# Turning most parts of H tiles 0 and 1 by DMA, and finding maxima over partitions with a TensorE transpose, in a quantised gated block

## The chip, the core and the metric

The kernel runs on one core of one Trainium2 chip. The metric is the device time of one execution in microseconds (us), lower is better. The engines are called here as the profile calls them: PE is the matrix engine, DVE the vector engine, ACT the scalar engine, POOL is GpSimd, SP issues all the DMAs. "SPq" is SP's queue; "PEld" is PE's loading of weights, which overlaps its matmuls.

## What is computed

```
x = x + tanh(g_xattn) * matmul(fake_quant(layernorm(x)), fake_quant(ctx))
h_in2 = layernorm(x)                               # 1024 rows x 1024
A, g  = quant_act(h_in2); Wg, Wu = quant_w(w_gate), quant_w(w_up)
h     = silu(A @ Wg.T * g) * (A @ Wu.T * g)        # 1024 rows x 2752
Am, gm = quant_act(h); Wd = quant_w(w_down)
x = x + tanh(g_ffn) * (Am @ Wd.T * gm)

def quant_act(v):            # blocks of 16 columns, fp8 rounding
    g = max(max|v| / (448 * 6), 1e-8)              # one maximum over the whole tensor
    vr = (v / g)[:, reorder]                       # the index may be the identity
    normal, last = vr[:, :-128], vr[:, -128:]
    q1 = fp8_block(last); q2 = fp8_block(last - q1)   # outliers in two steps
```

Two things matter here. quant_act needs one maximum over all elements before any element can be rounded, and each rounded tile has to be turned (rows to columns) before PE can multiply it.

## The kernel before, in words

The work goes in three stretches. The opening (to about 267 us of the span) does the attention part, quantises the activations and the first weights. The loop (to about 645 us) multiplies gate and up, makes h in units of 256 columns and stores it to DRAM (`h_d`), while the weights for the third stretch are quantised and turned into `big` (`wd_hi`, `wd_lo`). The last stretch, called here the down stretch, takes h back tile by tile: an H tile is 128 rows by 2752 columns, there are 8 of them, and tiles use two buffers in turn (`h_in[:, 0]`, `h_in[:, 1]`).

For each H tile, in the down stretch:
- `coef_unbound`, `keep_h_outliers` and `scale_h` (DVE, lines 1409, 1410, 1462, 1466) prepare one factor and one scale per block of 16.
- the tile is multiplied by its factors: by DVE part by part for tiles 0 and 1 (line 1477), by POOL in one go for tiles 2 to 7 (`h_times_coef`, line 626, after `hcoef_ready`).
- rounding (`start_part`, `end_part`): line 1478 makes a power of two `mg` from each element with integer operations, line 1479 keeps `mg` above a floor, lines 1485 and 1486 round by adding `mg` and taking it away, and line 1487 multiplies by the scale. The last part of a tile has the outliers as well (`quantise_twice`, twelve short instructions from line 1268 to 1275).
- the tile is split into two f16 numbers (hi and lo) and turned. Tiles 0 and 1 are cut in six parts of 3 or 4 blocks of 128 columns (`H_PARTS`). A part is turned by PE in f32 into a PSUM bank (`turn_h`, line 892), ACT copies it out as hi (`hi_part`, line 708), DVE takes hi from it and writes lo (`lo_part`, line 1178). Tiles 2 to 7 go in two halves of 11 blocks: ACT writes hi (line 838) and DVE lo (`lo_half`, line 1504) side by side in `nat_h`, and one DMA per half turns both (`turn_half`, line 503) into `amT`.
- PE multiplies each turned block three times (hi hi, hi lo, lo hi) for each of two halves of the output (`down`, line 1001): 132 matmuls of 128x512 per tile, 1056 in all. DVE adds the result to x1 (`finish`, line 1513, two instructions per tile), and SP stores it.

Each engine takes its instructions in the order in which they are written. DVE's order for tiles 0 and 1 is: start of part c, `lo_group` of part c-1, end of part c. For tiles 2 to 7: preparation, lo of the second half of the tile before, `finish(t-2)`, start and end of half 0, start of half 1, lo of half 0, end of half 1. PE's order is: turn the next part after the first output half of the present one. In the down stretch nothing but these orders and the semaphores decides what runs when.

The maximum over the whole tensor is found in three places with `partition_all_reduce` on POOL: for the flags that say whether an index is the identity (line 557), for the activations (line 568, then DVE line 1219) and for h (line 620, then DVE line 1434). Before each, DVE has one number per partition (`nfl`, `gmx`); after each, every partition has the maximum.

## Time and profile before

| | |
|---|---|
| median of 3 runs | 915.83 us (915.15 to 916.29) |
| the profiled execution | 915.4 us, of which the span from first to last instruction is 913.6 us |
| PE busy / DVE busy | 84% / 73% of the span |
| ACT, POOL busy | 29%, 36% |
| mean granted TensorE clock | 0.935 of full speed |

The shares are means over three stretches that have different limits. In the loop PE is busy without a gap, so it sets the time there; in the opening PE is seldom busy and DVE mostly is; the down stretch has both kinds of time in it. Granted clock 1.00 is 2.4 GHz, 0.50 is 1.2 GHz.

### The profile page before, as it was taken

To read this page: it belongs to the slowest core of one execution; us is meant where nothing else is said; L and a number is where in the kernel's file an instruction comes from. 1 tells how busy PE (TensorE), PEld (TensorE's weight loads), DVE (VectorE), ACT (ScalarE), POOL (GpSimd) and SP (SyncE) were. 2 spreads that over 40 slices of the span, in tenths; PEclk is the share of its full clock that TensorE was granted. 3 is DMA by queue.
4 is the path that set the end of the run, shared out by engine and by line. 5 is a ranking of instruction groups with operands and counts; after the bars stand their busy time and mean duration, and the time that the engine had idled before them with its cause. 6 is when DMAs were issued, how large, how long until landed. Compare 5 with 4: busy or idle time off the path is not lost.

```text
span 913.6 us, 10781 instructions
## 1 busy us (share of the span) xinstructions
PE 765.4 (84%) x3676; PEld 362.1 (40%) x3676; DVE 669.3 (73%) x1054; ACT 263.0 (29%) x344; POOL 328.0 (36%) x173
## 2 busy tenths in 40 slices
PE   0689200579999999999999999999699579999998
PEld 0233100445554444444444444444245234444443
DVE  5999789988757575757667576732787899999950
ACT  1973420331334342425343343420001001101010
POOL 1001136745216475757575665820000222012200
PEclk9999555689999999999999999999799879999999
DMA  7633300110036978898797979753100244764440
GB/s 289 215 103 155 117 21 0 47 56 21 28 111 121 237 161 200 181 211 188 182 207 170 232 166 237 159 116 136 68 31 33 85 101 126 171 171 125 101 110 24
DMA packets 178854, 119.01 MB, mean 130 GB/s; under 512 B 151808, under 2 KB 163072, under 8 KB 177792
## 3 DMA queue, kind: packets, MB, share of 16 engines
q1 hardware_dynamic: 178816, 118.53, 51.1%
q8 instruction: 20, 0.33, 0.1%
q14 instruction: 18, 0.15, 0.1%
HBM read 61.88 MB, written 19.66 MB: 89 GB/s over the span
## 4 chain that ended last, share of the span: by engine, by line
PE 70%; DVE 22%; issue 2%; ACT 2%; POOL 1%; DMA 1%; SPq 0%; DVEq 0%; ACTq 0%
PE acc L950 45%; PE acc L1001 22%; PE tb L892 2%; DVE bst L1070 2%; DVE big L1245 1%; DVE wbuf L1172 1%; DVE h_in L1244 1%; DVE h_in L1243 1%; PE acc L878 1%; DVE big L1100 1%; DVE h_in L1190 1%; DVE wbuf L1504 1%; DVE mid L1144 1%; DVE wbuf L1142 1%; DVE w_max L1160 1%
## 5 line engine op out<-in xcount | busy, mean ns | idle before, releaser
L950 PE MATMUL acc<-mid 128*128 128x512 f16 (+1 forms) x2112 | 448.9, 376 | 0.0
L950 PEld LDWEIGHTS acc<-mid 128*128 128x128 f16 x2112 | 207.5, 98 | 239.7 <-issue 2.7
L1001 PE MATMUL acc<-big,mid 128*128 128x512 f16 x1056 | 234.0, 383 | 17.1 <-DMA mid<-wbuf 15.8
L563 POOL TENSOR_TENSOR wbuf<-wbuf,w_inv 128x1024 f32<-128x1024 f32 (+1 forms) x68 | 128.5, 1894 | 157.6 <-DVE w_inv L1166 157.6
L1001 PEld LDWEIGHTS acc<-big,mid 128*128 128x128 f16 x1056 | 103.9, 99 | 142.4 <-issue 20.4
L602 POOL TENSOR_TENSOR h_in<-wbuf,h_in 128x1024 f16<-128x1024 f32 (+1 forms) x56 | 114.5, 2044 | 86.7 <-ACT h_in L799 86.5
L1316 DVE SCALAR_TENSOR_TENSOR h_out<-acc,gs,silu 128x256 f32<-128x256 f32 (+1 forms) x88 | 41.5, 471 | 114.0 <-ACT silu L757 87.7
L702 ACT ACTIVATE wbuf<-wbuf 128x1024 f32<-128x1024 f32 (+1 forms) x68 | 69.1, 1017 | 100.6 <-POOL wbuf L563 99.8
L1160 DVE TENSOR_REDUCE tb<-wbuf 128x64 f32<-128x1024 f32 (+1 forms) x56 | 65.5, 1169 | 43.3 <-DMA wbuf<-in_L_ffn_w_gate_dram 24.1
L626 POOL TENSOR_TENSOR h_in<-h_in,mid 128x2752 f32<-128x2752 f32 x6 | 29.3, 4885 | 181.5 <-DVE mid L1542 181.5
L799 ACT ACTIVATE h_in<-wbuf 128x1024 f16<-128x1024 f32 (+1 forms) x56 | 57.1, 1019 | 115.2 <-DVE wbuf L1172 115.2
L757 ACT ACTIVATE silu<-acc,gs 128x256 f32<-128x256 f32 (+1 forms) x88 | 40.1, 456 | 88.0 <-PE acc L950 88.0
L1172 DVE SCALAR_TENSOR_TENSOR wbuf<-wbuf,tb 128x1024 f32<-128x1024 f32 (+1 forms) x56 | 65.2, 1163 | 0.3
L838 ACT ACTIVATE wbuf<-h_in 128x1408 f16<-128x1408 f32 x12 | 16.5, 1377 | 149.1 <-DVE h_in L1487 88.9
L892 PE MATMUL tb<-ident,big 128*128 128x128 f32 x64 | 11.2, 349 | 56.9 <-DVE big L1275 50.8
L708 ACT ACTIVATE mid<-tb 128x512 f16<-128x512 f32 (+2 forms) x52 | 28.0, 575 | 97.0 <-PE tb L892 75.0
L1504 DVE TENSOR_TENSOR wbuf<-h_in,wbuf 128x1408 f16<-128x1408 f32 x12 | 42.3, 3528 | 1.8 <-ACT wbuf L838 1.4
L1178 DVE TENSOR_TENSOR mid<-tb,mid 128x512 f16<-128x512 f32 (+2 forms) x52 | 32.3, 654 | 12.4 <-ACT mid L708 12.2
L1321 DVE TENSOR_REDUCE hm<-h_out 128x256 f32 (+2 forms) x88 | 34.0, 387 | 2.7
L878 PE MATMUL acc<-mid,big 128*128 128x512 bf16 x128 | 31.2, 400 | 5.1 <-DVE big L1100 5.1
L892 PEld LDWEIGHTS tb<-ident,big 128*128 128x128 f32 x64 | 10.1, 184 | 57.7 <-DVE big L1275 51.3
L1166 DVE RECIPROCAL w_inv<-tb 128x64 f32<-128x64 f32 (+1 forms) x56 | 30.2, 539 | 1.9
(150 smaller groups left out, 595.2 us busy)
## 6 DMA issues: line engine op xcount, KB each, us to landing
h_in<-h_d SPq DMA_DIRECT2D x8, 1376.0 KB, 7.0
wbuf<-in_L_ffn_w_gate_dram SPq DMA_DIRECT2D x21, 512.0 KB, 4.5
wbuf<-in_L_ffn_w_up_dram SPq DMA_DIRECT2D x21, 512.0 KB, 4.1
h_d<-h_out SPq DMA_DIRECT2D x80, 128.0 KB, 3.4
wbuf<-in_L_ffn_w_down_dram SPq DMA_DIRECT2D x16, 512.0 KB, 4.4
wbuf<-in_ctx_dram SPq DMA_DIRECT2D x12, 512.0 KB, 4.7
big<-in_x_dram SPq DMA_DIRECT2D x8, 512.0 KB, 7.6
x_d<-big SPq DMA_DIRECT2D x8, 512.0 KB, 4.2
```

Of the source, the lines that this page charges most:

```text
L563: pool.tensor_tensor(w, w, spread(w_inv[0:rows, b, 0:cols // BLK]), ALU.mult).then_inc(w_scaled, 1)
L602: pool.tensor_tensor(nat[s % 4][:, H:H + cols], wbuf[:, s % 4, 0:cols], nat[s % 4][:, 0:cols], ALU.subtract)\
L702: act.activation(wbuf[0:rows, b, 0:cols], wbuf[0:rows, b, 0:cols], ACT.Copy, bias=MAGIC, scale=W_UP)\
L757: act.activation(silu[:, m % 2, 0:cols], acc[m % 4][:, 0:cols], ACT.Silu, scale=gs[:, 2:3]).then_inc(silu_done, 1)
L799: act.activation(nat[s % 4][:, 0:cols], wbuf[:, s % 4, 0:cols], ACT.Copy).then_inc(nat_hi, 1)
L878: pe.matmul(acc[pair(t) + hf][:], aT[:, k, t * P:(t + 1) * P], ctxq[:, b * KT + k, hf * MW:(hf + 1) * MW], start=(k == 0), stop=False)
L950: last = pe.matmul(acc[m % 4][:, 0:cols], left[:, k, s * P:(s + 1) * P], ring[:, slot, right, k, 0:cols], start=(k == 0 and left is a_hi a ...
L1001: last = pe.matmul(acc[2 * i + hf][:], amT[:, i, k // DH, left, k % DH, :], right[:, k, hf * MW:(hf + 1) * MW], start=(k == 0 and left == ...
L1160: dve.tensor_reduce(top, blocks(wbuf[0:rows, b, 0:cols]), AX_X, ALU.max, apply_absolute_value=True).then_inc(scale_step, 1)
L1172: dve.scalar_tensor_tensor(out=w, in0=w, scalar=MAGIC, in1=spread(block_scale(b, looped)[0:rows, 0:cols // BLK]), op0=ALU.subtract, op1=AL ...
L1316: dve.scalar_tensor_tensor(out=h_out[:, m % 2, 0:cols], in0=acc[m % 4][:, cols:2 * cols], scalar=gs[:, 2:3], in1=silu[:, m % 2, 0:cols], o ...
L1504: dve.tensor_tensor(nat_h[:, g, 1, :], h_in[:, i, g * DH * P:(g + 1) * DH * P], nat_h[:, g, 0, :], ALU.subtract)\
```

## The change

It has three parts.

1. `H_PARTS` becomes a list over all tiles: tile 0 in the same six parts as before, tile 1 in four parts of 5, 6, 5 and 6 blocks, tiles 2 to 7 in halves as before. Only the first two parts of tile 0 are still turned by PE (`PE_PARTS`). The other eight of tiles 0 and 1 are written as hi (ACT) and lo (DVE) into `nat_h`, and SP turns each with two DMAs (`turn_part`), one for hi and one for lo.
2. The floor on `mg` moves from DVE to ACT for all tiles: ACT computes Relu(mg * 2^20 - floor) in place (`floor_magic`), and DVE's two rounding instructions add the floor back. With that, the factors lose a power of two and the scales change their sign. In tiles 2 to 7 DVE's `finish(t-2)` now stands behind the start of half 0 and no longer before it.
3. The three calls of `partition_all_reduce` go. PE transposes the column of 128 numbers, spread over 128 columns, into a PSUM bank (`spread_max`), so that every partition has all 128 numbers, and DVE takes their maximum (one reduce). For the flags, DVE does this behind the first layernorm and no longer ahead of the work on the parameters.

POOL still multiplies H tiles 2 to 7.

```diff
-H_PARTS = (0, 3, 7, 11, 15, 19, DK)
-DG = len(H_PARTS) - 1
+H_CUTS = ((0, 3, 7, 11, 15, 19, DK), (0, 5, DH, 16, DK)) + ((0, DH, DK),) * (NT - 2)
+H_PARTS = [(t, slice(a, b)) for t, cuts in enumerate(H_CUTS) for a, b in zip(cuts, cuts[1:])]
+PE_PARTS = 2
+HALVES = sum(1 for t, ks in H_PARTS if t < 2)
...
+MAGIC_FLOOR = 1.5 * V_UP * 2.0**-6
...
@@ sync @@
+            def turn_part(n):
+                t, ks = H_PARTS[n]
+                sp.wait_ge(nat_h_lo, n - PE_PARTS + 1)
+                for v in range(2):
+                    sp.dma_start_transpose(turned_part(t, v, ks), nat_part(v, ks)).then_inc(part_turned[n], 16)
...
-            for t in range(2):
-                sp.wait_ge(turned, (t + 1) * DG + G_DOWN)
-                load_tile(t + 2, t)
+            for n in range(PE_PARTS, HALVES):
+                turn_part(n)
+                t, ks = H_PARTS[n]
+                if ks.stop == DK:
+                    sp.wait_ge(turned, G_DOWN + PE_PARTS)
+                    load_tile(t + 2, t)
...
@@ gpsimd: three calls go @@
-            pool.wait_ge(flag_step, 4)
-            pool.partition_all_reduce(nall[:], nfl[:], P, RMAX).then_inc(flag_step, 1)
...
-            pool.wait_ge(part_max, 1)
-            pool.partition_all_reduce(gall[:, 0:1], gmx[:, 0:1], P, RMAX).then_inc(all_max, 1)
...
-            pool.wait_ge(part_max, 2)
-            pool.partition_all_reduce(gall[:, 1:2], gmx[:, 1:2], P, RMAX).then_inc(all_max, 1)
...
@@ scalar @@
+            def floor_magic(n, ks):
+                mg = mgh[:, 0:min(ks.stop * P, I) - ks.start * P]
+                act.wait_ge(magic_made, n + 1)
+                act.activation(mg, mg, ACT.Relu, bias=floor_bias[:, 0:1], scale=V_UP).then_inc(magic_floor, 1)
+            floor_magic(0, H_PARTS[0][1])
+            for n, (t, ks) in enumerate(H_PARTS):
+                if n < PE_PARTS:
+                    hi_part(G_DOWN + n, (G_DOWN + n) % 4, turned_part(t, 0, ks), ks.stop - ks.start, P)
+                else:
+                    if n == PE_PARTS:
+                        act.wait_ge(nat_lo, UNITS_D * UNIT_PIECES)
+                    act.wait_ge(am_ready, n + 1)
+                    g = ks.start // DH
+                    if t in (1, 2) and ks.start == g * DH:
+                        for m in parts_in(t - 1, g):
+                            if m >= PE_PARTS:
+                                act.wait_ge(part_turned[m], 32)
+                    elif t > 2:
                         act.wait_ge(h_turned[g], 16 * (t - 2))
-                    act.activation(nat_h[:, g, 0, :], h_in[:, t % 2, g * DH * P:(g + 1) * DH * P], ACT.Copy).then_inc(nat_h_hi, 1)
+                    act.activation(nat_part(0, ks), h_in[:, t % 2, ks.start * P:ks.stop * P], ACT.Copy).then_inc(nat_h_hi, 1)
+                if n + 1 < len(H_PARTS):
+                    floor_magic(n + 1, H_PARTS[n + 1][1])
...
@@ tensor @@
+            def spread_max(column, out):
+                return pe.transpose(out, column.to_broadcast([P, P]), ident[:])
...
+            pe.wait_ge(flag_step, 4)
+            for i in range(2):
+                last = spread_max(nfl[:, i:i + 1], tb[3][:, i * P:(i + 1) * P])
+            last.then_inc(flag_step, 1)
...
+            pe.wait_ge(part_max, 1)
+            pe.wait_ge(lo_done, G_PRE)
+            spread_max(gmx[:, 0:1], tb[3][:, 0:P]).then_inc(all_max, 1)
...
+            pe.wait_ge(part_max, 2)
+            spread_max(gmx[:, 1:2], tb[3][:, 0:P]).then_inc(all_max, 1)
+            turn_h(0)
+            for n, (t, ks) in enumerate(H_PARTS):
+                if n < PE_PARTS:
+                    pe.wait_ge(lo_done, G_DOWN + n + 1)
+                elif t < 2:
+                    pe.wait_ge(part_turned[n], 32)
+                else:
+                    if ks.start == 0:
+                        pe.wait_ge(y_out, t - 1)
+                    pe.wait_ge(h_turned[ks.start // DH], 16 * (t - 1))
+                for hf in range(2):
+                    last = down(t % 2, hf, range(ks.start, ks.stop))
+                    if ks.stop == DK:
+                        last.then_inc(y_done, 1)
+                    if hf == 0 and n + 1 < PE_PARTS:
+                        turn_h(n + 1)
...
@@ vector @@
-            dve.wait_ge(flag_step, 5)
-            dve.tensor_copy(flag[:], nall[:]).then_inc(flags_ready, 1)
...
+            dve.wait_ge(flag_step, 5)
+            step(dve.tensor_reduce(nall[:], tb[3][:, 0:2 * P].rearrange("p (n c) -> p n c", n=2), AX_X, ALU.max))
+            dve.tensor_copy(flag[:], nall[:]).then_inc(flags_ready, 1)
...
+            step(dve.tensor_reduce(gall[:, 1:2], tb[3][:, 0:P], AX_X, ALU.max))
...
-                step(dve.tensor_scalar(mg.bitcast(I32), v.bitcast(I32), 0x7F800000, 0x00400000, ALU.bitwise_and, ALU.bitwise_or))
-                step(dve.tensor_scalar(mg, mg, 1.5 * V_UP * 2.0**-6, None, ALU.max))
-            def end_part(t, i, ks):
+                dve.tensor_scalar(mg.bitcast(I32), v.bitcast(I32), 0x7F800000, 0x00400000, ALU.bitwise_and, ALU.bitwise_or).then_inc(magic_made, 1)
+            def end_part(n, i, ks):
                 cs = slice(ks.start * P, min(ks.stop * P, I))
                 v, mg = h_in[:, i, cs], mgh[:, 0:cs.stop - cs.start]
-                step(dve.scalar_tensor_tensor(out=v, in0=v, scalar=1.0 / V_UP, in1=mg, op0=ALU.mult, op1=ALU.add))
-                step(dve.tensor_tensor(v, v, mg, ALU.subtract))
+                dve.wait_ge(magic_floor, n + 1)
+                step(dve.scalar_tensor_tensor(out=v, in0=mg, scalar=MAGIC_FLOOR, in1=v, op0=ALU.add, op1=ALU.add))
+                step(dve.scalar_tensor_tensor(out=v, in0=mg, scalar=MAGIC_FLOOR, in1=v, op0=ALU.add, op1=ALU.subtract))
...
+            def lo_h(n):
+                t, ks = H_PARTS[n]
+                if n < PE_PARTS:
+                    g = G_DOWN + n
+                    lo_part(g, g % 4, turned_part(t, 0, ks), turned_part(t, 1, ks), ks.stop - ks.start, P)
+                else:
+                    dve.wait_ge(nat_h_hi, n - PE_PARTS + 1)
+                    dve.tensor_tensor(nat_part(1, ks), h_in[:, t % 2, ks.start * P:ks.stop * P], nat_part(0, ks), ALU.subtract)\
+                        .then_inc(nat_h_lo, 1)
...
+            for n, (t, ks) in enumerate(H_PARTS):
                 i = t % 2
-                reorder_max(t, i)
-                coef_unbound(t, i, step)
-                keep_h_outliers(i)
-                dve.tensor_scalar(h_coef[:, i, :], h_coef[:, i, :], gs[:, 6:7], None, ALU.min).then_inc(hcoef_ready, 1)
-                scale_h(t, i)
-                if t == 2:
-                    lo_group(1, DG - 1)
+                if ks.start == 0:
+                    reorder_max(t, i)
+                    if t >= 1:
+                        if t >= 2:
+                            coef_unbound(t, i, step)
+                        keep_h_outliers(i)
+                        if t >= 2:
+                            dve.tensor_scalar(h_coef[:, i, :], h_coef[:, i, :], gs[:, 6:7], None, ALU.min).then_inc(hcoef_ready, 1)
+                        scale_h(t, i)
+                    if t >= 2:
+                        lo_h(n - 1)
+                if t == 0 and ks.stop == DK:
+                    keep_h_outliers(0)
+                start_part(t, i, ks)
+                if n == 0:
+                    dve.tensor_scalar(gs[:, 5:6], gs[:, 3:4], th[:, 1:2], W_DOWN, ALU.mult, ALU.mult)
+                    step(dve.tensor_scalar(gs[:, 7:8], gs[:, 4:5], -1.0 / FP8_MAX, None, ALU.mult))
+                    dve.wait_ge(hmax_done, (NU + 1) * NT)
+                    scale_h(0, 0)
+                elif t < 2 or ks.start > 0:
+                    lo_h(n - 1)
                 else:
-                    lo_half(t - 1, 1 - i, 1)
-                finish(t - 2, i)
-                start_part(t, i, slice(0, DH))
-                end_part(t, i, slice(0, DH))
-                start_part(t, i, slice(DH, DK))
-                lo_half(t, i, 0)
-                end_part(t, i, slice(DH, DK))
-            lo_half(NT - 1, 1, 1)
+                    finish(t - 2, i)
+                end_part(n, i, ks)
+            lo_h(len(H_PARTS) - 1)
```

What the order of instructions is on DVE in the middle of tile 0 (the part of blocks 7 to 10; `mid` is `mg` or `amT`, `tb` is the PSUM bank of the turned part), before:

```order
L1477 SCALAR_TENSOR_TENSOR h_in<-mid,gs,h_in 128x512
L1478 TENSOR_SCALAR mid<-h_in 128x512 [waits dve_step]
L1479 TENSOR_SCALAR mid<-mid 128x512 [waits dve_step]
L1178 TENSOR_TENSOR mid<-tb,mid 128x512 [waits hi_done,dve_step]
L1485 SCALAR_TENSOR_TENSOR h_in<-h_in,mid 128x512
L1486 TENSOR_TENSOR h_in<-h_in,mid 128x512 [waits dve_step]
L1487 TENSOR_TENSOR h_in<-h_in,mid 128x512 [waits dve_step]
```

and now:

```order
L1530 SCALAR_TENSOR_TENSOR h_in<-mid,gs,h_in 128x512
L1531 TENSOR_SCALAR mid<-h_in 128x512 [waits dve_step]
L1555 TENSOR_TENSOR wbuf<-h_in,wbuf 128x512 [waits nat_h_hi]
L1538 SCALAR_TENSOR_TENSOR h_in<-mid,h_in 128x512 [waits magic_floor]
L1539 SCALAR_TENSOR_TENSOR h_in<-mid,h_in 128x512 [waits dve_step]
L1540 TENSOR_TENSOR h_in<-h_in,mid 128x512 [waits dve_step]
```

One instruction of the part is gone (line 1479), the lo instruction reads `h_in` and `wbuf` in place of a PSUM bank, and the rounding waits for ACT (`magic_floor`).

On DVE from the preparation of tile 2 to its first rounding, before:

```order
L1409 TENSOR_SCALAR mid<-hm 128x172
L1410 RECIPROCAL mid<-mid 128x172 [waits dve_step]
L1462 TENSOR_SCALAR mgo_a<-h_in,gs 128x128 [waits dve_step]
L1542 TENSOR_SCALAR mid<-mid,gs 128x172 [waits dve_step]
L1466 TENSOR_SCALAR mid<-hm,gs 128x172
L1178 TENSOR_TENSOR mid<-tb,mid 128x384 [waits hi_done,dve_step]
L1513 SCALAR_TENSOR_TENSOR mid<-acc,gs,mid 128x512 [waits y_done,x1_loaded0]
L1513 SCALAR_TENSOR_TENSOR mid<-acc,gs,mid 128x512 [waits y_done]
L1478 TENSOR_SCALAR mid<-h_in 128x1408 [waits h_scaled]
L1479 TENSOR_SCALAR mid<-mid 128x1408 [waits dve_step]
L1485 SCALAR_TENSOR_TENSOR h_in<-h_in,mid 128x1408 [waits dve_step]
```

and now:

```order
L1461 TENSOR_SCALAR mid<-hm 128x172
L1462 RECIPROCAL mid<-mid 128x172 [waits dve_step]
L1515 TENSOR_SCALAR mgo_a<-h_in,gs 128x128 [waits dve_step]
L1577 TENSOR_SCALAR mid<-mid,gs 128x172 [waits dve_step]
L1519 TENSOR_SCALAR mid<-hm,gs 128x172
L1555 TENSOR_TENSOR wbuf<-h_in,wbuf 128x768 [waits nat_h_hi,dve_step]
L1531 TENSOR_SCALAR mid<-h_in 128x1408 [waits h_scaled]
L1564 SCALAR_TENSOR_TENSOR mid<-acc,gs,mid 128x512 [waits y_done,x1_loaded0]
L1564 SCALAR_TENSOR_TENSOR mid<-acc,gs,mid 128x512 [waits y_done]
L1538 SCALAR_TENSOR_TENSOR h_in<-mid,h_in 128x1408 [waits magic_floor]
```

The lo instruction of tile 1's last part (line 1178 before, 1555 now) is larger and has two inputs in SBUF, and `finish` (1513 before, 1564 now) has moved behind the first instruction that waits for POOL (`h_scaled`).

On PE from the end of the loop to tile 0's second part, before:

```order
L892 MATMUL tb<-ident,h_in 128x128 x3
L1001 MATMUL acc<-big,mid 128x512 x9
L892 MATMUL tb<-ident,h_in 128x128 x4
L1001 MATMUL acc<-big,mid 128x512 x21
L892 MATMUL tb<-ident,h_in 128x128 x4
L1001 MATMUL acc<-big,mid 128x512 x24
L892 MATMUL tb<-ident,h_in 128x128 x4
```

and now:

```order
L883 MATMUL tb<-ident,gmx 128x128
L934 MATMUL tb<-ident,h_in 128x128 x3
L1051 MATMUL acc<-big,mid 128x512 x9
L934 MATMUL tb<-ident,h_in 128x128 x4
L1051 MATMUL acc<-big,mid 128x512 x1047
```

The transpose of the maxima stands ahead, two turns of parts are left of twelve, and all other matmuls of the stretch stand in one row.

## Rows read from the trace of the kernel before

**Rows 1.** The page: costliest groups, busy us and mean ns, idle before and its releaser.

```profile
L1001 PE MATMUL acc<-big,mid 128*128 128x512 f16 x1056 | 234.0, 383 | 17.1 <-DMA mid<-wbuf 15.8
```

**Rows 2.** Stretches before tile 2's matmuls: busy us, clock, DMA share, GB/s.

```profile
core 0: us, PE busy (x) PEld busy (x) DVE busy (x) ACT busy (x) POOL busy (x), PEclk, DMA share, GB/s
...
682.00:714.00 32.00, 30.79 (x153) 15.24 (x152) 26.59 (x56) 3.37 (x6) 0.00 (x0) 1.00 0.12 45
714.00:736.00 22.00, 6.75 (x33) 2.87 (x31) 18.67 (x20) 1.87 (x2) 4.89 (x1) 0.71 0.43 123
```

**Rows 3.** Waits, 640 to 760 us: total us, times, longest.

```profile
PE acc L1001 <- DMA mid<-wbuf: 15.8, 2, 15.5
...
DVE mid L1178 <- ACT mid L708: 9.2, 10, 1.7
```

**Rows 4.** Timeline (start us, us): the maximum of h and the first parts.

```profile
646.66 0.16 DVE L1418 TENSOR_REDUCE gmx<-gpart 128x1 f32<-128x4 f32 x1
...
647.37 0.15 DVE L1434 TENSOR_SCALAR gs<-gall 128x1 f32<-128x1 f32 x1 [0.23 <-POOL gall L620]
...
651.46 0.56 DVE L1487 TENSOR_TENSOR h_in<-h_in,mid 128x384 f32<-128x384 f32 x1
...
652.27 0.87 PE L892 MATMUL tb<-ident,h_in 128*128 128x128 f32 x3 [7.18 <-DVE h_in L1487]
...
654.38 4.01 PE L1001 MATMUL acc<-big,mid 128*128 128x512 f16 x9 [1.25 <-DVE mid L1178]
```

**Rows 5.** Groups by shape on DVE, 640 to 720 us: busy us, mean ns.

```profile
L1485 DVE SCALAR_TENSOR_TENSOR h_in<-h_in,mid 128x512 f32<-128x512 f32 x8 | 5.5, 682 | 0.0
L1479 DVE TENSOR_SCALAR mid<-mid 128x512 f32<-128x512 f32 x8 | 3.4, 427 | 0.3
...
L1479 DVE TENSOR_SCALAR mid<-mid 128x384 f32<-128x384 f32 x2 | 0.7, 361 | 0.1
```

**Rows 6.** Timeline: tile 2 from DVE's first instruction to its matmuls.

```profile
713.60 0.25 DVE L1409 TENSOR_SCALAR mid<-hm 128x172 f32<-128x172 f32 x1
...
715.87 4.89 POOL L626 TENSOR_TENSOR h_in<-h_in,mid 128x2752 f32<-128x2752 f32 x1 [68.53 <-DVE mid L1542]
716.03 0.56 DVE L1178 TENSOR_TENSOR mid<-tb,mid 128x384 f16<-128x384 f32 x1
...
720.79 0.89 DVE L1478 TENSOR_SCALAR mid<-h_in 128x1408 int32<-128x1408 int32 x1 [2.88 <-POOL h_in L626]
...
722.65 1.63 DVE L1485 SCALAR_TENSOR_TENSOR h_in<-h_in,mid 128x1408 f32<-128x1408 f32 x1
...
727.69 1.38 ACT L838 ACTIVATE wbuf<-h_in 128x1408 f16<-128x1408 f32 x1 [12.89 <-DVE h_in L1487]
...
731.00 3.31 SPq L503 DMA_TRANSPOSE mid<-wbuf  x1
...
736.28 16.31 PE L1001 MATMUL acc<-big,mid 128*128 128x512 f16 x66 [15.54 <-DMA mid<-wbuf]
```

**Rows 7.** Timeline: lo of tile 2's second half beside POOL, and PE afterwards.

```profile
741.21 4.88 POOL L626 TENSOR_TENSOR h_in<-h_in,mid 128x2752 f32<-128x2752 f32 x1 [20.45 <-DVE mid L1542]
741.38 6.19 DVE L1504 TENSOR_TENSOR wbuf<-h_in,wbuf 128x1408 f16<-128x1408 f32 x1
...
752.86 37.51 PE L1001 MATMUL acc<-big,mid 128*128 128x512 f16 x173 [0.27 <-DMA mid<-wbuf]
```

**Rows 8.** DMA issues: operation, times, median us from issue to landing.

```profile
big<-h_in SPq DMA_TRANSPOSE x48, 3.8
```

**Rows 9.** Timeline of the opening.

```profile
4.64 3.97 SPq L327 DMA_DIRECT2D big<-in_x_dram x8
...
9.45 0.17 DVE L1052 CAST flag<-nall 128x2 int32<-128x2 f32 x1 [2.87 <-POOL nall L557]
...
10.91 9.58 DVE L1070 BATCH_NORM_STATS2 bst<-big 128x6 f32<-128x512 f32 x16
```

**Rows 10.** The last two of the eight loads of x: us from issue to landing.

```profile
DMA to landing us min/median/max: 9.5/9.9/10.3
```

More of the change, by code:

```diff
@@ L29 @@
 AX_X = mybir.AxisListType.X
-RMAX = bass.bass_isa.ReduceOp.max
 P = 128
@@ L265, in gated_block @@
         am_ready = sem("am_ready")
+        magic_made = sem("magic_made")
+        magic_floor = sem("magic_floor")
         nat_h_hi = sem("nat_h_hi")
         nat_h_lo = sem("nat_h_lo")
+        part_turned = [sem(f"part_turned{n}") for n in range(HALVES)]
         h_turned = [sem(f"h_turned{g}") for g in range(2)]
@@ L301, in unit_tile, with part_of, parts_in, nat_part @@
             return u * NT + (2 * NT + s)
-        def halves_before(t):
-            return 2 * (t - 2)
-        def parts_before(t):
-            return DG * t if t < 2 else 2 * DG + halves_before(t)
+        def part_of(t, k):
+            return next(n for n, (at, ks) in enumerate(H_PARTS) if at == t and ks.start <= k < ks.stop)
+        def parts_in(t, g):
+            return [n for n, (at, ks) in enumerate(H_PARTS) if at == t and ks.start // DH == g]
+        def nat_part(v, ks):
+            g = ks.start // DH
+            return nat_h[:, g, v, (ks.start - g * DH) * P:(ks.stop - g * DH) * P]
+        def turned_part(i, v, ks):
+            g = ks.start // DH
+            return amT[:, i, g, v, ks.start - g * DH:ks.stop - g * DH, :]
         def loads_before(b, u):
@@ L989, in _, with turn_h @@
                     unit(2 * it + (jj + 1), 1 - jj)
-            def turn_h(t, c):
-                pe.wait_ge(am_ready, t * DG + c + 1)
-                g = G_DOWN + t * DG + c
-                turn_piece(h_in[:, t, :], P, range(H_PARTS[c], H_PARTS[c + 1]), g, g % 4)
+            def turn_h(n):
+                pe.wait_ge(am_ready, n + 1)
+                t, ks = H_PARTS[n]
+                turn_piece(h_in[:, t, :], P, range(ks.start, ks.stop), G_DOWN + n, (G_DOWN + n) % 4)
             def down(i, hf, ks):
@@ L1218, in _ @@
             dve.wait_ge(all_max, 1)
+            step(dve.tensor_reduce(gall[:, 0:1], tb[3][:, 0:P], AX_X, ALU.max))
             step(dve.tensor_scalar(gs[:, 0:1], gall[:, 0:1], 1.0 / GDIV, TINY, ALU.mult, ALU.max))
@@ L1408, in coef_unbound @@
                 mx, coef = hm[:, t, :], h_coef[:, i, :]
-                link(dve.tensor_scalar(coef, mx, H_SMALL, 1.0 / (FP8_MAX * V_UP), ALU.max, ALU.mult))
+                link(dve.tensor_scalar(coef, mx, H_SMALL, 1.0 / FP8_MAX, ALU.max, ALU.mult))
                 link(dve.reciprocal(coef, coef))
@@ L1464, in scale_h @@
             def scale_h(t, i):
-                step(dve.tensor_scalar(h_scale[:, i, :], hm[:, t, :], gs[:, 7:8], TINY, ALU.mult, ALU.max))
+                step(dve.tensor_scalar(h_scale[:, i, :], hm[:, t, :], gs[:, 7:8], -TINY, ALU.mult, ALU.min))
             def start_part(t, i, ks):
```

68 lines of the change are left out of this document (8 added, 60 removed).

## The prediction

> **What bounds the kernel now.** I read the page first, then the waits and the stretches of the down part, then its timeline. The group of line 1001 on the page holds all 1056 matmuls of the down stretch, and its idle time has one main cause, a DMA that turns H [rows 1]. The waits say that this is two waits, one of 15.5 us [rows 3]. The stretch from 714 to 736 us shows it: PE is busy for 6.75 of 22 us while DVE is busy for 18.67 [rows 2]. From 752.86 on PE runs at 37.51 / 173 = 0.217 us per matmul and does not wait again before the end [rows 7]. So the end follows from the moment at which the second half of tile 2 reaches PE, 752.86, and everything ahead of that in the down stretch is a race for it.
>
> Who runs that race is seen in the timeline of tile 2 [rows 6]. PE starts tile 2 when a DMA lands, that DMA is issued behind DVE's lo, and DVE's chain for tile 2 starts at 713.60, right behind its work on tiles 0 and 1. PE had nothing to do by then. So the sum is made along DVE: how much earlier does it come to 713.60, and how much earlier to the issue at 731.00? The second half follows the first at the same distance, since between them stand the same outliers, the same preparation of tile 3 and the same POOL instruction. What DVE saves inside tile 2 and later, beyond that point, only makes tiles wait for PE.
>
> **The change part by part.**
>
> *DVE's waits for turned parts.* In tiles 0 and 1 DVE waits ten times for ACT's hi, 9.2 us in all [rows 3], because PE turns a part only between the matmuls of the part before. Eight of ten such parts no longer pass PE: hi comes from ACT straight from `h_in`, and DVE has the next part's first two instructions in between. Laying the instructions of both engines one behind the other with the durations of the rows, I get for what is left: 0.6 and 1.8 at the two parts that PE still turns, and where ACT has copy and floor to do in one part, 0.1 to 0.5 each until the floor is there (0.60 + 0.1 for a floor of 512 columns, estimated from ACT's 1.38 for 1408 [rows 6]), 1.9 together. So 4.3 stay and **4.9** go. Bounds: none of the 1.9 stays (6.8), or each floor takes 0.4 longer and all of it shows (about 1.3).
>
> *The floor.* Twelve instructions of line 1479 leave DVE in tiles 0 and 1: eight at 0.43, two at 0.36, two a little shorter [rows 5], each with 0.03 to the next: **5.2**. The two rounding instructions keep their size; one changes from two to three operands, and line 1485, which is of that form, takes 0.68 for 512 [rows 5], as the other does within 0.01.
>
> *Six parts into four in tile 1.* Line 1485 takes 0.68 for 512 and 1.63 for 1408 columns [rows 5, 6], so 1.06 ns per column and 0.14 fixed. Two parts fewer with six instructions each save about **1.8**, with bounds 1.2 and 2.4.
>
> Together DVE comes to tile 2 some 11.9 us earlier, at 701.7 by the old clock.
>
> *Around tile 2's factors.* POOL multiplies for 4.89, and DVE then had 2.88 idle, because lo (0.56) and `finish` lay in POOL's shadow [rows 6]. Now the lo of tile 1's last part has two inputs in SBUF. What that does beside POOL is seen at tile 2's second half: lo of 1408 columns, alone no longer than a rounding instruction of that size (1.63), takes 6.19 and ends 1.48 behind POOL [rows 6, 7]; the 0.56 one that reads PSUM ran at full speed beside POOL [rows 6]. So the new one, of 768 columns, ends 0.9 behind POOL: **+0.8**, and if it were free, 0. The Trainium skill ("SBUF — State Buffer", section "SBUF: two separate sides") has the same as a rule: GpSimd and a DVE instruction with two SBUF inputs exclude each other for a whole instruction, which speaks against this part of the change. By the rule the term is 0.8, by sizes alone it would be nothing and the time 0.8 lower; the trace agrees with the rule.
>
> `finish` now stands between the start and the end of half 0. It takes 1.3 there, then some 0.3 until the floor is ready, and the 0.93 of line 1479 are gone: **+0.7**, between 0.4 and 1.2. For the lo of half 0, DVE waits for ACT's copy where it had line 1479 to do; that is even within 0.1. From 11.9 the gain shrinks to 10.4.
>
> *The maximum of h.* From the end of `gmx` (646.82) to DVE's next instruction took 0.55 with POOL [rows 4]. Now: DVE to PE 0.25, as between 652.02 and 652.27; one f32 transpose, bounded by the 0.87 of three [rows 4], say 0.45; a reduce of 128 numbers and the semaphores 0.35. That makes 1.05, so **+0.5**, with bounds 0 and +1.0. The maximum of the activations, in the opening's chain, costs the same once more: **+0.5**.
>
> *The opening.* DVE waited 2.87 for POOL's answer on the flags ahead of anything on x, then ran sixteen statistics without a gap from 10.91 to 20.49, 1.2 per tile, the last tile from 19.3. That tile's load was issued at 8.2 and took 10.3 [rows 9, 10], so it is there at 18.5 and the statistics can end 0.8 earlier. The flags' reduce falls into a wait for ACT behind the layernorm. **-0.8**, between 0 and -0.85.
>
> *The turns as DMAs.* A pair of DMA transposes with 6 or 8 blocks each lands 3.8 after its issue in the median of single ones [rows 8], and 44 blocks in one DMA took 5.3 (731.00 to 736.28) [rows 6]. I take 4.0 for a pair of 4 to 6 blocks, bounds 2.7 and 5.3. They are on PE's path, not DVE's. PE will wait for parts: for the third part of tile 0 about 2 us, for the first of tile 1 some 2 to 4 (its lo comes behind tile 0's outliers, and its DMAs are issued behind the load of H tile 2 on SP's queue), and for the last of tile 1, whose lo ends behind POOL at 710.3 (701.7 + 0.5 for the maximum, 2.3 to POOL's start, 4.9, and 0.9). That one lands at 714.3, its 36 matmuls end at 722.1. Tile 2 lands at 736.3 - 10.4 + 0.5 = 726.4. So PE still waits 4.3 there, and that cover hides the turns' cost; beyond it, each us costs one. The transposes that leave PE (0.15 each) save nothing for the same reason.
>
> Sum: -4.9 - 5.2 - 1.8 + 0.8 + 0.7 + 0.5 + 0.5 - 0.8 = -10.2. The profiled execution took 915.4 (span 913.6), 0.4 under the median of the runs, so 905.2, or 905.6 from the median. I put 905.4.
>
> **The rivals.**
>
> *The floor on ACT comes late (0.14).* The Trainium skill ("ScalarE: Activation LUTs", "Rules for kernel authors") sends relu and max to VectorE; its figures, an estimate of 0.3 + 0.83 ns per element, make 0.7 for a floor of 512 columns. The sum above has nearly that already. The mechanism goes by rows: line 1479 takes 0.43 on DVE [rows 5], ACT needs 1.38 for 1408 in its plain copy [rows 6], and in each part it has both the copy and the floor, in a row. If a floor with its two hand-overs takes 0.4 more than I took, nine of them lie open up to tile 2's first rounding: +3.6, 909. For it: ACT's floor reads its bias from memory. Against: ACT is nearly idle here.
>
> *PE becomes the bound in tiles 0 and 1 (0.12).* After a wait PE's clock falls: the nine matmuls at 654.38 took 0.446 each, against 0.217, behind 7 us of little work [rows 4, 7], so a restart costs 2.0. One restart at the last part of tile 1 moves 722.1 to 724.1, still inside the cover. With pairs that land at 5.3 and two restarts that add up it is 727 to 729: +1 to +3, 906 to 908.
>
> *The gain is larger (0.08).* No floor ever lies open and the maxima cost nothing: 1.9 + 1.0 more, 902.4.
>
> *Slower than before (0.04).* The short waits of PE in front of every part keep its clock at the lower level. All 255 matmuls behind the first nine would take 0.446 in place of 0.217, 58 us more. It needs less: when about 120 of them do, tile 1 ends 27 us late, at 749, PE takes up tile 2 some 13 us later than before, at full clock its first half ends at 763.5 and not at 752.9, and the time is about 926. It decides from the point at which tile 1 ends after 738. Against it: from 682 to 714 PE was busy for 30.79 of 32 us, so it waited now and then, and kept 1.00 of the clock [rows 2].
>
> *Nothing changes (0.02).* Something that I don't see sets tile 2's landing, such as the load of H tile 2 or 3 behind the turns.
>
> **How the numbers follow.** The main case has 0.60 and, with its bounds added as they would fall together, reaches from 902.5 to 908. The range takes in the larger gain and the late floor: 901.5 to 909.5, which leaves out less than 2 in 10. A measurement of this kernel tells some 0.2% (1.8 us) from no change. Faster by over that: all cases but the last two, less a little for a mishap outside this list, 0.93; within 0.2%: 0.03; slower: 0.04.
>
> **What would show it.** Right: DVE starts tile 2 near 702, with no wait over 0.6 behind the second part of tile 0; the lo of tile 1's last part takes about 5.5 beside POOL; PE starts tile 2 near 726 after a wait of some 4 us, and is without a gap from about 742 on; the statistics end near 19.7; the two maxima take near 1.0. Wrong: DVE waiting for `magic_floor` over 0.5 a part, PE at the lower clock for most of tile 0 or 1, turn pairs that take over 5.3, or a gap of PE later than 745.

## The result, and the profile after

The changed kernel takes 901.47 us (median of 4 runs, 900.67 to 901.84); the kernel before took 916.06 in the same rounds. The ratio is 0.9841, with a 95% interval from 0.9824 to 0.9858: faster by 14.6 us. The prediction was 905.4 with a range from 901.5 to 909.5, so the sign was right, but the gain, forecast at 10.2, was 4.4 larger than said, and the measured time lies just under the lower end of the range. The profiled execution took 901.84, its span is 900.1 (before: 915.4 and 913.6).

I read the new page and the waits first. In the page's costliest groups (columns as in [rows 1]) the matmuls of the down stretch and the new floor on ACT read:

```profile
L1051 PE MATMUL acc<-big,mid 128*128 128x512 f16 x1056 | 235.6, 387 | 9.9 <-DMA mid<-wbuf 8.7
...
L852 ACT ACTIVATE mid<-mid,floor_bias 128x1408 f32<-128x1408 f32 (+7 forms) x22 | 24.7, 1124 | 56.4 <-DVE mid L1531 56.4
```

PE's idle time in the stretch fell from 17.1 [rows 1] to 9.9 us. The waits of the changed kernel between 640 and 760 us (as [rows 3]: in total, times, longest) say where it and DVE's waits went:

```profile
PE acc L1051 <- DMA mid<-wbuf: 8.7, 4, 3.6
...
DVE mid L1229 <- ACT mid L731: 2.7, 2, 2.3
...
DVE h_in L1538 <- ACT mid L852: 2.0, 8, 0.4
...
DVE wbuf L1555 <- ACT wbuf L871: 1.3, 2, 0.7
```

The one wait of 15.5 at tile 2 has become 3.6, beside three smaller ones in tiles 0 and 1, and DVE's ten waits for a turned part are two. The timeline of tile 2 (start and duration in us) answers to [rows 6]:

```profile
698.55 0.25 DVE L1461 TENSOR_SCALAR mid<-hm 128x172 f32<-128x172 f32 x1
...
700.81 4.88 POOL L649 TENSOR_TENSOR h_in<-h_in,mid 128x2752 f32<-128x2752 f32 x1 [103.14 <-DVE mid L1577]
700.98 5.52 DVE L1555 TENSOR_TENSOR wbuf<-h_in,wbuf 128x768 f16<-128x768 f32 x1
...
707.34 1.47 ACT L852 ACTIVATE mid<-mid,floor_bias 128x1408 f32<-128x1408 f32 x1 [7.84 <-DVE mid L1531]
708.84 1.63 DVE L1538 SCALAR_TENSOR_TENSOR h_in<-mid,h_in 128x1408 f32<-128x1408 f32 x1 [0.22 <-ACT mid L852]
...
710.67 7.94 PE L1051 MATMUL acc<-big,mid 128*128 128x512 f16 x36 [1.24 <-DMA mid<-wbuf]
...
716.94 3.30 SPq L525 DMA_TRANSPOSE mid<-wbuf  x1
```

DVE comes to tile 2 at 698.55, not at 713.60. To split that into opening and down stretch, I took the long last pieces of each kernel's chain of waits (start, us, and the matmuls run together). Before:

```profile
266.95 378.15 PE acc L950 x1752
...
752.86 156.88 PE acc L1001 x726
```

After:

```profile
264.07 378.15 PE acc L1000 x1752
...
722.23 173.95 PE acc L1051 x792
```

The long middle piece takes 378.15 in both and starts 2.9 earlier now. Before, PE's last wait ended at 752.86 [rows 7], 107.8 behind the end of the long piece (645.10); from there on the rest, 726 matmuls, takes 156.88. After, PE's last matmul ends at 896.18, so the same 726, at the same 156.88, begin at 739.3, 97.1 behind 642.22. So the spans' difference of 13.5 is **2.9 from the opening and 10.7 from the down stretch**. The forecast had -0.3 for the opening (-0.8 for the flags, +0.5 for the maximum of the activations) and -9.9 for the down stretch. The opening is what I got wrong. The split is good to less than a us only: in the nine kernels here that take both opening maxima on PE the long piece starts anywhere from 263.40 to 264.87, in the two that take both on POOL at 266.95 and 267.19.

### The profile page after: what moved, and what is told of

Read it like the earlier page. It is cut to its first block, busy times and chain, and to the rows that moved or that the text cites. A ratio compares the mean times of both kernels' runs of the same rounds, so it can differ in the third digit from the quotient of the medians.

```text
span 900.1 us, 10681 instructions
## 1 busy us (share of the span) xinstructions
PE 762.3 (85%) x3638; PEld 358.4 (40%) x3643; DVE 657.4 (73%) x1021; ACT 287.0 (32%) x364; POOL 326.1 (36%) x171
## 4 chain that ended last, share of the span: by engine, by line
PE 68%; DVE 24%; ACT 2%; issue 2%; DMA 2%; POOL 1%; SPq 1%; DVEq 0%; ACTq 0%
PE acc L1000 46%; PE acc L1051 20%; DVE bst L1118 2%; PE tb L934 2%; DVE big L1297 1%; DVE wbuf L1223 1%; DVE big L1148 1%; DVE h_in L1296 1%; DVE h_in L1241 1%; DVE w_max L1211 1%; DMA mid<-wbuf 1%; DVE h_in L1295 1%; DVE mid L1195 1%; DVE wbuf L1193 1%; DVE h_in L1539 1%
## 5 line engine op out<-in xcount | busy, mean ns | idle before, releaser
L1555 DVE TENSOR_TENSOR wbuf<-h_in,wbuf 128x1408 f16<-128x1408 f32 (+4 forms) x20 | 53.0, 2652 | 5.7 <-ACT wbuf L871 5.5
L871 ACT ACTIVATE wbuf<-h_in 128x1408 f16<-128x1408 f32 (+4 forms) x20 | 22.1, 1105 | 107.2 <-DVE h_in L1327 62.3
L852 ACT ACTIVATE mid<-mid,floor_bias 128x1408 f32<-128x1408 f32 (+7 forms) x22 | 24.7, 1124 | 56.4 <-DVE mid L1531 56.4
L731 ACT ACTIVATE mid<-tb 128x512 f16<-128x512 f32 (+2 forms) x42 | 22.4, 578 | 43.0 <-PE tb L979 21.7
L1564 DVE SCALAR_TENSOR_TENSOR mid<-acc,gs,mid 128x512 f32<-128x512 f32 x16 | 11.4, 739 | 31.0 <-PE acc L1051 31.0
```

What stands on the lines that cost most here:

```text
L1555: dve.tensor_tensor(nat_part(1, ks), h_in[:, t % 2, ks.start * P:ks.stop * P], nat_part(0, ks), ALU.subtract)\
```

## The experiments

Each kernel was timed in five rounds (4 to 8 executions) against the kernel before; gains are against the median of the kernel before in the same rounds (915.63 to 916.49). "Slower than the changed kernel" compares with its 901.47, which comes from other rounds; reckoned by the gains, such differences change by up to 0.4.

**The maxima.** First theory (P): something behind the removed `partition_all_reduce` of the activations was worth more than the reduce's own path. The kernel before with only this maximum moved to PE:

```diff
-            pool.wait_ge(part_max, 1)
-            pool.partition_all_reduce(gall[:, 0:1], gmx[:, 0:1], P, RMAX).then_inc(all_max, 1)
...
+            pe.wait_ge(part_max, 1)
+            pe.wait_ge(lo_done, G_PRE)
+            spread_max(gmx[:, 0:1], tb[3][:, 0:P]).then_inc(all_max, 1)
...
+            step(dve.tensor_reduce(gall[:, 0:1], tb[3][:, 0:P], AX_X, ALU.max))
```

> The kernel before, with only the maximum of the activations found by a TensorE transpose and a DVE reduce, in place of POOL's partition_all_reduce. Theory P (after a partition_all_reduce POOL cannot start its next ordinary instruction for some 7 us, and in the opening 2.9 us of that lie open): the path of the maximum is 0.3 longer, POOL starts its first product about 2.9 earlier, net about 2 us faster, 914. Rival Q (the gain in the opening comes from the earlier start, by which DVE and POOL meet otherwise): 0.3 slower, 916.4. The prediction's own term was 0.5 slower.

Measured: 914.2, ratio 0.9974 (0.9964 to 0.9985), a gain of 2.3 where the prediction had a loss of 0.5. Its long piece starts at 265.43, 1.5 earlier than before.

The changed kernel, with a `partition_all_reduce` of `gmx` into a column that nothing reads. It takes nothing away and nobody waits for its result; only POOL's order has one instruction more:

```diff
+            pool.wait_ge(part_max, 1)
+            pool.partition_all_reduce(unused[:, 0:1], gmx[:, 0:1], P, RMAX)
             for what, n in (("coef", 0), ("coef", 1), ("coef", 2), ("piece", 4), ("piece", 5), ("scale", 0), ("scale", 1),
```

> The changed kernel as it is, and POOL does a partition_all_reduce of the activation maxima as well, whose result nobody reads. The path of the maximum is untouched. Theory P: POOL's first product starts 2 to 3 us later and the end moves by about that, 903.5 to 904.4. Rival Q: nobody waits for it, 901.5.

Measured: 903.3 (0.9854, 0.9838 to 0.9869), 1.8 slower than the changed kernel. The timeline (idle before and its releaser in brackets) shows the mechanism; the kernel before:

```profile
121.44 0.38 POOL L568 PARTITION_ALL_REDUCE gall<-gmx  x1 [20.45 <-DVE gmx L1215]
128.95 6.16 POOL L576 TENSOR_TENSOR big<-big,h_in 128x1024 f32<-128x1024 f32 x3 [7.14 <-issue]
...
135.07 5.24 POOL L563 TENSOR_TENSOR wbuf<-wbuf,w_inv 128x1024 f32<-128x1024 f32 x2
...
138.45 2.42 DVE L1243 TENSOR_SCALAR h_in<-big 128x1024 int32<-128x1024 int32 x1
```

The changed kernel:

```profile
126.06 5.71 POOL L598 TENSOR_TENSOR big<-big,h_in 128x1024 f32<-128x1024 f32 x3 [26.03 <-DVEq L1348]
...
131.73 4.72 POOL L587 TENSOR_TENSOR wbuf<-wbuf,w_inv 128x1024 f32<-128x1024 f32 x2
...
137.45 0.68 DVE L1295 TENSOR_SCALAR h_in<-big 128x1024 int32<-128x1024 int32 x1
```

The changed kernel with the unused reduce:

```profile
120.56 0.38 POOL L612 PARTITION_ALL_REDUCE unused<-gmx  x1 [20.44 <-DVE gmx L1270]
128.00 6.16 POOL L600 TENSOR_TENSOR big<-big,h_in 128x1024 f32<-128x1024 f32 x3 [7.06 <-issue]
```

The reduce is shown with 0.38 us, but POOL's next instruction starts 7.1 behind its end, "issue" in the brackets: it waits for nothing that the profile shows. Its operands are ready long before (DVE makes the last coefficient at 125.61 in the changed kernel, and POOL starts at 126.06 there). In the kernels with the reduce POOL starts 1.9 to 2.3 later behind that coefficient than in the changed one. DVE meets this delay at its second bit operation (line 1243 before, 1295 after): before, POOL's pair of multiplications still runs beside it, until 140.31, and it takes 2.42; after, the pair is over at 136.45, and it takes 0.68. That 1.7 is the gain. A reduce that stands where POOL has nothing to do should cost nothing; the same unused instruction at the maximum of h:

```diff
+            pool.wait_ge(part_max, 2)
+            pool.partition_all_reduce(unused[:, 1:2], gmx[:, 1:2], P, RMAX)
             def h_times_coef(t, i):
```

> The changed kernel, and POOL does an unused partition_all_reduce of the h maxima, after which it is idle for some 57 us. Theory P: the gap behind it is covered by that idleness, 901.5. If a partition_all_reduce costs time whatever follows it, about 2 us more.

Measured: 901.49 (0.9839, 0.9825 to 0.9852): nothing. These are the same rounds as those of the 903.3, so the two unused reduces differ by 1.8 through their place alone. The same view of this kernel:

```profile
644.55 0.38 POOL L648 PARTITION_ALL_REDUCE unused<-gmx  x1 [46.45 <-DVE gmx L1475]
700.99 4.88 POOL L654 TENSOR_TENSOR h_in<-h_in,mid 128x2752 f32<-128x2752 f32 x1 [56.05 <-DVE mid L1582]
```

POOL idles 56 us behind it anyway. The flags, back on POOL in the changed kernel, with DVE's wait for them ahead of the statistics as before:

```diff
+            pool.wait_ge(flag_step, 4)
+            pool.partition_all_reduce(nall[:], nfl[:], P, RMAX).then_inc(flag_step, 1)
...
+            dve.wait_ge(flag_step, 5)
+            dve.tensor_copy(flag[:], nall[:]).then_inc(flags_ready, 1)
```

> The changed kernel with the flags' maximum back on POOL and ahead of DVE's work on the parameters. The statistics then end 0.8 later; if that reaches the end, 902.3. If the earlier start of DVE is swallowed later in the opening, 901.5.

Measured: 902.6 (0.9855, 0.984 to 0.987), 1.1 slower where the term says 0.8; its long piece starts at 265.21, also 1.1 later. Now all three maxima together, first moved alone in the kernel before:

> The kernel before, with all three maxima found by TensorE and DVE, and nothing else changed. Theory P: the opening gains 2.9, the maximum of h costs 0.3, so 913.4. By the prediction's terms (0.5 and 0.5 lost, 0.8 won) and by rival Q without the down stretch: 916.1, no change.

Measured: 913.03 (0.9965, 0.9951 to 0.9978), a gain of 3.5; by the prediction's terms it would have been none (-0.8 + 0.5 + 0.5 = +0.2). Then all three undone in the changed kernel:

> The changed kernel with all three maxima over partitions taken by POOL's partition_all_reduce again, as before the change; turns, floor and parts stay changed. Theory P (the missed term of the opening is what POOL does behind a partition_all_reduce; the down stretch went as forecast): the opening gives its 2.9 us back and the maximum of h takes 0.3 less, so 901.5 + 2.9 - 0.3 = 904.1 (903.4 to 904.9), POOL's first multiplication of the activations stands some 7 us behind its reduce, and PE's last loop of the middle stretch starts near 267 us. Theory Q (the terms of the prediction for the maxima hold and the surplus came from the down stretch): 901.5 + 0.8 - 0.5 - 0.5 = 901.3.

Measured: 904.88 (0.9879, 0.9864 to 0.9894), 3.4 slower than the changed kernel, at the upper end of P and far from Q. Its long piece starts at 267.19, and its first multiplication on POOL 6.97 behind the end of the reduce, as P said.

**The down stretch.** Its terms, one at a time, but for the move of `finish`, which was not undone by itself. The floor back on DVE (the main lines of the edit):

```diff
-                dve.tensor_scalar(mg.bitcast(I32), v.bitcast(I32), 0x7F800000, 0x00400000, ALU.bitwise_and, ALU.bitwise_or).then_inc(magic_made, 1)
+                step(dve.tensor_scalar(mg.bitcast(I32), v.bitcast(I32), 0x7F800000, 0x00400000, ALU.bitwise_and, ALU.bitwise_or))
+                step(dve.tensor_scalar(mg, mg, V_UP, MAGIC_FLOOR, ALU.mult, ALU.max))
...
```

> The changed kernel with the floor back on DVE for all tiles (the two-input rounding instructions stay). Theory of the sum: DVE gets twelve... here ten floor instructions of tiles 0 and 1 back (about 4.9 us) and loses its waits for ACT's floor (2.0), and in tile 2's first half 0.9 in place of 0.2, with finish no longer covering anything: tile 2 lands 3.6 later, 905.1. Rival: PE is the bound in tiles 0 and 1 and the floor does not matter, 901.5.

Measured: 905.01 (0.9885, 0.987 to 0.99), 3.5 slower. Tile 1 in six parts, `H_CUTS` with `(0, 3, 7, 11, 15, 19, DK)` in place of `(0, 5, DH, 16, DK)`:

> The changed kernel with tile 1 in six parts as tile 0. Theory of the sum: two parts more cost DVE 1.8, which reaches the end, 903.3. Rival: smaller parts land sooner and PE waits less, 901.5 or below.

Measured: 904.35 (0.9877, 0.9862 to 0.9893), 2.9 slower by the medians, 1.7 by the spans (901.8 against 900.1). DVE starts tile 2 there at 701.28, 2.7 later, of which 0.3 come from the opening; the lo of the last part, now 384 columns, takes 5.12 beside POOL in place of 5.52 and gives 0.4 back.

Both of them together leave of the down stretch's change the turns alone:

> The changed kernel with the floor back on DVE and tile 1 back in six parts: of the change of the down stretch only the turns by DMA are left. Theory P (the three terms add up once the turns are DMAs): 901.5 + 3.5 for the floor + 1.8 to 2.9 for the parts = 906.8 to 907.9, which puts the turns alone 5.1 to 6.2 below the kernel that changed the maxima alone (913.0). Theory Q (the turns only pay together with the faster DVE): 910 or above.

Measured: 907.77 (0.9918, 0.9905 to 0.9932), where P had 906.8 to 907.9. So with the turns as DMAs the terms nearly add up. They don't without them. The changed kernel with all parts of tiles 0 and 1 turned by PE (`PE_PARTS = 12`, six parts in tile 1), floor on ACT and maxima on PE kept:

> The changed kernel with tiles 0 and 1 in six parts each, all turned by PE as before; floor on ACT, maxima on TensorE. Theory of the sum, against the six-part kernel at 903.3: DVE's waits for turned parts come back (9.2 in place of 4.7), and lo of tile 1's last part reads PSUM and is not held by POOL (0.8 back): 907. Rival: who turns does not matter, since PE has cover ahead of tile 2, 903.3 or less.

Measured: 912.74 (0.9965, 0.9953 to 0.9977), where I had expected 907. That is a gain of 3.2 and no more than the maxima alone gave (3.5): of the floor's 5.2 us of DVE's time little or nothing reaches the end. (The traces, from the end of the long piece to the last 726 matmuls, have 107.4 here, 108.4 with the maxima alone and 107.8 before, so at most about 1.) Its waits between 640 and 760 us:

```profile
PE acc L1047 <- DMA mid<-wbuf: 16.3, 2, 15.9
DVE mid L1225 <- ACT mid L727: 12.8, 10, 2.0
...
DVE mid L1527 <- POOL h_in L645: 4.2, 1, 4.2
```

Most of what DVE saves comes back as waiting: 12.8 for turned parts in place of 9.2 [rows 3], and 4.2 for POOL at tile 2 in place of 2.88 [rows 6], where `finish` no longer fills the time. The chain of the kernel before, in tile 0, shows why:

```profile
663.36 0.44 PE tb L892 x4
663.80 5.18 PE acc L1001 x24
668.98 0.44 PE tb L892 x4
669.41 5.18 PE acc L1001 x24
```

A part of four blocks costs PE 5.62 (24 matmuls and a turn), and DVE, whose waits sit in this ring, could not go faster than that there. In the changed kernel's chain the same stretch is DVE and ACT alone:

```profile
660.64 0.73 ACT mid L852
661.40 0.70 DVE h_in L1538
662.13 0.70 DVE h_in L1539
662.85 0.69 DVE h_in L1540
663.54 0.67 DVE h_in L1530
664.70 0.73 ACT mid L852
```

A part comes every 4.06 there (660.64 to 664.70), and the floor is in the chain itself (0.73 in the rows above): DVE waits for it in six of the ten parts, 0.2 to 0.4 each.

**A faster version.** Two runs test whether I now know what sets the end. If it is DVE's chain at tile 2, the POOL instruction there is too dear. H tile 2 multiplied by DVE, POOL from tile 3 on:

```diff
-                if t >= 2:
-                    dve.wait_ge(h_scaled, t - 1)
+                if t >= 3:
+                    dve.wait_ge(h_scaled, t - 2)
                 else:
                     coef = spread(h_coef[:, i, cs.start // BLK:cs.stop // BLK])
...
```

> The changed kernel, but H tile 2 is multiplied by DVE, as tiles 0 and 1 are, and POOL takes tiles 3 to 7. Theory P (DVE's chain up to tile 2's first half still sets the end): lo of tile 1's last part takes 0.9 in place of 5.5 and the multiplication of the half adds 1.6, minus an and that stays, so DVE gets to the first bit operation of tile 2 some 3 us earlier and tile 2 reaches PE near 719 in place of 722.2: 898.2 (897.3 to 899.0), and nothing is gained beyond about 3.6, since PE then has no wait left there. Theory Q (PE, with its waits for single parts, sets the end by now): 901.5, with a wait at tile 2 that ends where it did, or a longer wait elsewhere.

Measured: 899.17 (0.9819, 0.9806 to 0.9832), a gain of 2.3 where I expected 3.3, just outside the range of P. The timeline from tile 2 on, and the last piece of the chain behind it:

```profile
700.72 0.96 DVE L1555 TENSOR_TENSOR wbuf<-h_in,wbuf 128x768 f16<-128x768 f32 x1
...
710.60 1.61 DVE L1530 SCALAR_TENSOR_TENSOR h_in<-mid,gs,h_in 128x1344 f32<-128x1344 f32 x1
...
720.01 14.40 PE L1051 MATMUL acc<-big,mid 128*128 128x512 f16 x66 [2.82 <-DMA mid<-wbuf]
...
725.13 6.19 DVE L1555 TENSOR_TENSOR wbuf<-h_in,wbuf 128x1408 f16<-128x1408 f32 x1
...
736.56 3.63 PE L1051 MATMUL acc<-big,mid 128*128 128x512 f16 x16 [2.15 <-DMA mid<-wbuf]
```

```profile
736.56 156.88 PE acc L1051 x726
```

The lo of 768 columns takes 0.96, not 5.52. I had left out that the multiplication of the second half (1.61) stands ahead of the first half's lo, so the first half reached PE at 720.01 and not near 719. And the end is set by the second half, whose own lo of 1408 columns still takes 6.19 beside POOL. So, in this version, DVE's lo was put ahead of the factors that release POOL:

```diff
                         keep_h_outliers(i)
                         if t >= 3:
+                            lo_h(n - 1)
                             dve.tensor_scalar(h_coef[:, i, :], h_coef[:, i, :], gs[:, 6:7], None, ALU.min).then_inc(hcoef_ready, 1)
                         scale_h(t, i)
-                    if t >= 2:
+                    if t == 2:
                         lo_h(n - 1)
```

> The kernel that multiplies tile 2 on DVE (899.2), and from tile 3 on DVE's lo of the half before stands ahead of the factors that release POOL, so that it has no POOL instruction beside it. Theory P (with tile 2 on DVE the end follows from the second half of tile 2, whose lo takes 6.19 beside POOL at 725.13 and lets PE wait 2.15 at 736.56): the lo takes 1.63, the half lands some 4 us earlier, PE goes on at 734.4 without a wait, and the time is 899.2 - 2.15 = 897.0 (896.5 to 897.7). Theory Q (the second half isn't the bound, or its DMA, not its lo, sets it): 899.2.

Measured: 897.68 (0.9801, 0.9788 to 0.9814), within P's range, 3.8 below the changed kernel and 18.2 below the kernel before. The same places of its timeline:

```profile
718.35 21.99 PE L1051 MATMUL acc<-big,mid 128*128 128x512 f16 x94 [4.33 <-DMA mid<-wbuf]
...
722.91 1.63 DVE L1555 TENSOR_TENSOR wbuf<-h_in,wbuf 128x1408 f16<-128x1408 f32 x1
...
724.84 4.88 POOL L649 TENSOR_TENSOR h_in<-h_in,mid 128x2752 f32<-128x2752 f32 x1 [130.80 <-DVE mid L1578]
```

The lo takes 1.63 and PE has no wait left behind 718.35. The medians differ by 1.5, less than the wait of 2.15 that went. In this trace PE takes 21.99 for the first 94 matmuls of tile 2, 0.234 each, where the version before took 14.40 for 66, 0.218 each: the granted clock is 0.57 from 718.3 to 722 us, so a slow start gives back some 1.5. (The trace is also the fastest of its five executions, 1.0 under their median: PE was back at full clock sooner in tile 0, and DVE waited 1.7 and not 2.7 for turned parts. That 1.0 is not the edit's.) PE's wait of 4.33 stands ahead of this start, so what would come next is tile 2's first half; that was not tried.

## Why the prediction was right and where it was wrong

*The opening: the step that failed.* The step is the term for the maximum of the activations. The prediction costed the maximum of the activations as +0.5, on the path from `gmx` to DVE's next instruction, and wrote that it "costs the same once more". On that path it was +0.34 (from the start of the instruction that makes `gmx` to the start of the next on DVE that needs the maximum, 1.24 before and 1.58 after in the chains). But the step looked only at who waits for the reduce, not at what stands behind it on POOL. There POOL's next instruction came 7.1 after the reduce, the row for that was in the trace of before, and at this place POOL has work that DVE runs into. Taking the reduce away gave 1.5 to 1.8 at the start of PE's long piece (265.43 against 266.95; 264.07 against 265.85 with the unused reduce), and 2.3 and 1.8 in the medians, so the term is about -1.6 to -2 in place of +0.5. For the flags the term was right in place and near in size: in the timeline of the changed kernel the statistics end at 19.76, where 19.7 was forecast, and undoing it costs 1.1, not 0.8.

```profile
19.76 0.71 DVE L1123 BATCH_NORM_AGGREGATE mv<-bst 128x2 f32<-128x12 f32 x8
```

Together the opening was -2.9 and not -0.3. That is 2.6 of the 3.3 by which the difference of the spans (13.5) exceeds the sum (10.2); the rest is the down stretch. The medians differ by another 1.1, about what single times of one kernel differ by (900.67 to 901.84, 915.15 to 916.3).

*DVE to tile 2.* Forecast 11.9 earlier without the maxima, measured 12.4: from the first use of the maximum of h, at 647.37 [rows 4], to 713.60 [rows 6] before, and from 644.75 to 698.55 after.

```profile
643.78 0.16 DVE L1470 TENSOR_REDUCE gmx<-gpart 128x1 f32<-128x4 f32 x1
...
644.75 0.15 DVE L1487 TENSOR_SCALAR gs<-gall 128x1 f32<-128x1 f32 x1
```

The waits that were to stay, 4.3, are 4.2 (2.7 for the two parts that PE turns, 1.5 for floors). Right. But its split into 4.9 for waits, 5.2 for the floor and 1.8 for the parts read as three independent savings, and they are not: PE's turning held DVE to 5.62 a part, the floor without the turns saves 0.3 by the medians (912.74 against 913.03), and only behind the turns does it give its 3.5. The sum was right because all three were in the change.

*Tile 2's factors.* The lo of the last part took 5.52 beside POOL where 5.5 was said, and the next instruction came at 706.43, 0.74 behind POOL's end (+0.8 forecast). By the Trainium skill ("SBUF — State Buffer", section "SBUF: two separate sides") the two exclude each other for a whole instruction; the trace agrees: the same kind of instruction took 0.96 in the run without POOL beside it. `finish` and the floor behind it cost 0.55 (2.41 from the first bit operation to the first rounding, 1.86 before), where 0.7 was said, with a wait of 0.22 for the floor. The issue of tile 2's transpose came 11.4 earlier against the maximum, where 10.4 were forecast: 0.5 of that is DVE's way to tile 2, the rest lies in these two terms and in the way from the first rounding to the issue, which is 0.25 shorter.

*The maximum of h.* Forecast +0.5, measured +0.26: from the end of `gmx` to the next factor 0.55 before [rows 4] and 0.81 after (643.94 to 644.75), with the transpose of 128x128 at 0.29 where 0.45 was said.

*PE.* The pair of the last part landed 4.1 behind its issue (706.53 to 710.67) where 4.0 was taken, PE waited 3.6 at tile 2 where 4.3 was forecast, and there is no wait behind it. The forecast moved both halves of tile 2 by the same amount; in fact the first half's 66 matmuls take longer now and end the race themselves. The stretches of the changed kernel (columns as in [rows 2], the granted clock is the last number but two):

```profile
722.00:728.00 6.00, 5.77 (x14) 2.05 (x15) 5.52 (x17) 1.38 (x1) 0.85 (x1) 0.50 0.20 72
728.00:740.00 12.00, 12.00 (x57) 5.43 (x56) 11.71 (x7) 1.47 (x1) 4.03 (x1) 1.00 0.46 95
```

The granted clock is 0.50 for 6 us, the lower of the two levels, and PE does 14 matmuls where it does 28 at the full one; so the first half ends at 739.3, when the second half is there already (its issue at 733.54 and the 5.16 that the DMA of the first took make 738.7). A slow start isn't new: before, behind the wait of 15.5, the granted clock was low too, here in columns us, PE busy, granted clock, DMA share and GB/s.

```profile
738.00:740.00 2.00, 2.00 (x6) 0.50 0.00 0
```

The 66 matmuls took 16.31 then [rows 6] and take 17.07 now (722.23 to 739.3); from the first half's start to the second's it is 16.58 before and 17.07 after, so this costs 0.5 that the forecast didn't have. The down stretch adds up: +0.26 for the maximum, -11.4 for the issue, +0.5 here, -10.7 in all. The rival in which the low clock became the rule for tiles 0 and 1 didn't happen: behind the start of tile 0 (granted 0.50 from 650 to 655 us, 0.87 to 660) it shows once more, from 685 to 690 us (0.70).

*The rivals.* The late floor (909), PE as the bound (906 to 908) and the slower case (926) didn't occur; the floor's waits were 0.2 to 0.4 a part, as the sum had them, and a floor of 512 columns took 0.71 to 0.72 on ACT, where the sum had 0.70. The larger gain (902.4) came nearest to the time, but for another reason: the floor did lie open, and the maxima paid because of POOL's order, which it didn't name.

What stays open is what POOL does in the 7.1 us behind a `partition_all_reduce`; the profile shows no instruction there and no run here looked inside. The flags' reduce of the kernel before has such a gap ahead of it as well: it starts 5.61 behind the end of POOL's instruction before it, and DVE's wait of 2.87 for the flags [rows 9] is that gap's end.

```profile
9.04 0.37 POOL L557 PARTITION_ALL_REDUCE nall<-nfl  x1 [5.61 <-issue]
```

## What to carry to other kernels

Cost a removed instruction twice: once for those who wait for its result, and once for what stands behind it on its own engine, from the end of its row to the start of the next one. A gap marked "issue" behind an instruction can be that instruction's cost: here it went when the instruction went. When two engines work in a ring, time saved on one shows only once the other's round is no longer the slower one, so terms of one stretch shouldn't be added before asking which of them opens the ring. And an instruction with two SBUF inputs is cheap or dear by its place: ahead of the release of POOL's multiplication it took 1.63, beside it 6.19.
